# Cross-attention with a routed feed-forward on one core: the feed-forward two token tiles behind the attention, a third x2 buffer, row maxima and one product of k's rotation kept in PSUM

## What is computed

```python
x = x + xattn(layernorm(x), ctx, ctx, pos, Wq, Wk, Wv, Wo)
x = x + ffn(layernorm(x), A, B, Wq_w, keys)

# xattn: 32 query heads of 16, 8 key/value heads (each used by 4 query heads), 16 batches of 64 x 64 scores
q = rope(query @ Wq);  k = rope(key @ Wk);  v = value @ Wv        # rope(a) = a*cos + rotate_half(a)*sin
out = softmax(q k^T / sqrt(16)) v @ Wo

# ffn: a low-rank feed-forward with a router over 64 experts of rank 8, 16 of them taken
scores = (x @ Wq_w.T) @ keys.T
gate   = softmax over the 16 largest scores, zero elsewhere       # (token, 64)
out    = ((x @ A.T) * gate, each gate value for 8 columns) @ B.T * 2
```

## Time and profile before

| | before |
|---|---|
| median of 3 runs | 194.94 us (194.22 to 195.06) |
| the profiled execution's own time | 194.51 us |
| its span, first to last instruction | 192.8 us |
| TensorE (PE) busy | 173.4 us, 90% |
| VectorE (DVE) busy | 151.0 us, 78% |
| ScalarE (ACT) busy | 89.9 us, 47% |
| GpSimd (POOL) busy | 86.8 us, 45% |
| moved by DMA | 11.3 MB, most of it in the first 25 us |
| chain that ended last, by engine | TensorE 51%, VectorE 29%, waiting for nothing visible 12%, ScalarE 5% |

### The profile page before, as it was taken

How to read it: one execution, slowest core, us unless ns; L and a number is a source line. 1 busy time by engine, 2 the same in 40 slices (tenths; PEclk the granted TensorE clock), 3 DMA queues, 4 the chain that set the end, 5 groups by cost and what they waited for, 6 DMA issues and landing times.

```text
span 192.8 us, 4096 instructions
## 1 busy us (share of the span) xinstructions
PE 173.4 (90%) x1446; PEld 130.6 (68%) x1446; DVE 151.0 (78%) x391; ACT 89.9 (47%) x206; POOL 86.8 (45%) x109
## 2 busy tenths in 40 slices
PE   7998899968997999989997999989999896788884
PEld 2656474745984878667975878667866784567764
DVE  2588959997899887988799597986798497645671
ACT  3767789537252741546352732456233614412310
POOL 5698888699489105740267104810363020220300
PEclk9999999999999999999999999999999999999999
DMA  5999501020010302001010100010000100000102
GB/s 187 327 389 401 231 2 56 2 51 7 3 54 0 109 3 56 0 3 54 3 56 0 58 0 0 2 53 5 3 0 0 58 0 0 5 2 0 54 37 75
DMA packets 5332, 11.32 MB, mean 59 GB/s; under 512 B 688, under 2 KB 944, under 8 KB 5056
## 3 DMA queue, kind: packets, MB, share of 16 engines
q1 hardware_dynamic: 5024, 10.79, 16.0%
q10 hardware_dynamic: 288, 0.27, 0.4%
HBM read 8.95 MB, written 2.10 MB: 57 GB/s over the span
## 4 chain that ended last, share of the span: by engine, by line
PE 51%; DVE 29%; issue 12%; ACT 5%; DVEq 0%; ACTq 0%
PE ps_w L1013 8%; DVE neg_top L734 8%; PE ps_w L1008 6%; PE ps_t L1021 6%; PE ps_w L1009 5%; PE ps_s L1104 4%; DVE m_split L744 3%; PE ps_s L1087 3%; PE ps_t L1026 3%; PE ps_w L1163 3%; DVE o_s L752 3%; DVE q_a L717 2%; DVE o_t L761 2%; DVE q_b L719 2%; PE ps_w L1155 2%
## 5 line engine op out<-in xcount | busy, mean ns | idle before, releaser
L313 POOL TENSOR_TENSOR late<-late,gate 128x512 f32<-128x512 f32 x7 | 8.0, 1145 | 48.8 <-issue 32.1
L734 DVE TENSOR_REDUCE neg_top<-ps_s 128x8 f32<-128x512 f32 x32 | 19.8, 676 | 0.7 <-PE ps_s L1068 0.7
L298 POOL TENSOR_TENSOR oT_lo<-o_n,oT_hi 128x512 fp32r<-128x512 f32 x8 | 10.3, 1285 | 21.0 <-ACT oT_hi L491 21.0
L483 ACT ACTIVATE eT<-ps_s 128x512 f32<-128x512 f32 x32 | 17.0, 600 | 4.2 <-PE ps_s L1093 4.2
L1008 PE MATMUL ps_w<-am_hi,x2T_hi 128*128 128x288 f32 x52 | 15.4, 319 | 1.6 <-ACT x2T_hi L504 1.6
L1008 PE MATMUL ps_w<-b_hi,zT_hi 128*128 128x512 f32 (+1 forms) x32 | 12.8, 405 | 3.9 <-DVE q_b L719 2.0
L1009 PE MATMUL ps_w<-am_lo,x2T_hi 128*128 128x288 f32 x52 | 14.2, 296 | 0.0
L1008 PE MATMUL ps_w<-wo_hi,oT_hi 128*128 128x512 f32 x32 | 13.3, 414 | 0.9 <-ACT oT_hi L491 0.8
L476 ACT ACTIVATE mT<-ps_t 128x256 fp32r<-128x256 f32 x8 | 3.1, 384 | 23.2 <-PE ps_t L1077 23.2
L1009 PE MATMUL ps_w<-wo_lo,oT_hi 128*128 128x512 f32 x32 | 12.6, 395 | 0.0
L1009 PE MATMUL ps_w<-b_lo,zT_hi 128*128 128x512 f32 (+1 forms) x32 | 12.1, 381 | 0.0
(11 more groups left out here) (187 smaller groups left out, 528.2 us busy)
## 6 DMA issues: line engine op xcount, KB each, us to landing
x_sb<-x SPq DMA_DIRECT2D x8, 256.0 KB, 6.6
cT_in<-cT SPq DMA_DIRECT2D x7, 256.0 KB, 2.9
out<-res SPq DMA_DIRECT2D x7, 256.0 KB, 2.0
wq_sb<-wq SPq DMA_DIRECT2D x4, 256.0 KB, 6.2
late<-wo SPq DMA_DIRECT2D x1, 1024.0 KB, 8.4
am_sb<-aT SPq DMA_DIRECT2D x1, 1024.0 KB, 7.7
b_sb<-bT SPq DMA_DIRECT2D x1, 1024.0 KB, 6.3
wkv_sb<-wkv SPq DMA_DIRECT2D x1, 512.0 KB, 4.5
```

What stands on the lines that cost most here:

```text
L298: pool.tensor_tensor(oT_lo[:], o_n[:].rearrange("p (b r q) -> p r b q", b=2, r=REP), oT_hi[:].bitcast(F32), ALU.subtract).then_inc(oT_lo_o ...
L483: act.activation(eT[:, c].rearrange("p b n -> p (b n)"), ps_s[:, c, :], ACT.Exp)\
L734: dve.tensor_reduce(neg_top[:, :, b, HALF_H * half:HALF_H * (half + 1)], ps_s[:, 2 * (1 - b) + half, :].rearrange("p (r h k) -> p r h k", ...
```

## The change

The computation stays the same. `step(i)` on all engines now runs the feed-forward of token f = i - 2 (none in step 1); g = i - 1 is the token whose x2 is turned and split in that step. `last()` therefore has four feed-forwards (z = 4, a = 5, m = 6, l = 7) instead of three, in a new order on each engine. x2 gets a third buffer in the part of `wq_sb` that raw q no longer needs. x2 is turned into bank `ps_t1` (before: `ps_t0`); some banks of the last tokens differ. `neg_top` becomes 32 columns of the scores' own third bank, with the order of the two inner indices swapped, and the second maximum waits for the first; `k_a` becomes 128 free columns of `ps_w1`. In `first()` on ScalarE `x_raw(0)` comes earlier. Two splits of B move on GpSimd. The stores of tokens 0 and 1 move behind later loads. 12 warming multiplications instead of 18. On GpSimd `last()` only gains `gated(z)` in front; `gated(a)` and `deviation2(m)` stand before `o_low(l)` as they did. On ScalarE, in `last()` not shown below, `q_high(l)` comes behind `z_first(z)`, `o_high(m)` behind the exponentials of l and `expert_exps(a)`, then `o_high(l)`, `x2_centre(m)`, `z_second(a)`, `x2_high(m)`, `z_high(a)`.

```diff
-WARM = 18
+WARM = 12
...
-        k_a, k_b, k_r = sb("k_a", [P, KV]), sb("k_b", [P, KV]), sb("k_r", [P, KV])
+        k_b, k_r = sb("k_b", [P, KV]), sb("k_r", [P, KV])
...
-        neg_top = sb("neg_top", [P, 2, 2, KVH])
...
+        neg_top = ps_s[:, 2, 0:4 * KVH].rearrange("p (b h r) -> p b h r", b=2, r=2)
+        k_a = ps_w1[:, 2 * KV:3 * KV]
...
         def x2_of(t):
-            return x2[:, t % 2, :] if t < T - 1 else xh[:]
+            return (x2[:, 0, :], x2[:, 1, :], wq_sb[:, 0, :])[t % 3]
+
+        def x2T_of(t):
+            return (x2T_hi, x2T_lo) if t < T - 1 else (xT_hi, xT_lo)
+
+        def x2T_bank(t):
+            return ps_t0 if t == T - 1 else ps_t1
+
+        def y_bank(t):
+            return ps_w1[:] if t < T - 1 else ps_s[:, 2, :]
 
...
             load_c(4)
             load_x(6)
             load_c(5)
-            store(0)
             load_x(7)
             load_c(6)
-            store(1)
+            store(0)
             load_c(7)
-            for t in range(2, T - 1):
+            for t in range(1, T - 1):
...
-                split_lo(b_lo, b_sb, b_hi, b_h, b_l, 0)
                 rotated_q(2)
                 c_low(3)
-                split_lo(b_lo, b_sb, b_hi, b_h, b_l, 1)
+                k_blocks(2, 0)
+                k_blocks(2, 1)
 
             def step(i):
-                f, n, p = i - 1, i + 1, i + 2
+                f, n, p = i - 2, i + 1, i + 2
                 if p + 1 < T:
                     deviation1(p + 1)
-                deviation2(f)
-                if i == 1:
-                    k_blocks(n, 0)
-                    k_blocks(n, 1)
-                gated(f)
-                if i == 1:
-                    split_lo(b_lo, b_sb, b_hi, b_h, b_l, 2)
-                    split_lo(b_lo, b_sb, b_hi, b_h, b_l, 3)
+                if f >= 0:
+                    gated(f)
+                else:
+                    for k in range(2):
+                        split_lo(b_lo, b_sb, b_hi, b_h, b_l, k)
+                deviation2(i - 1)
                 o_low(i)
                 k_blocks(p, 0)
                 k_blocks(p, 1)
+                rotated_q(p)
                 if p + 1 < T:
                     c_low(p + 1)
-                rotated_q(p)
+                if f < 0:
+                    for k in range(2, DK):
+                        split_lo(b_lo, b_sb, b_hi, b_h, b_l, k)
 
             def last():
-                l, m, a = T - 1, T - 2, T - 3
+                l, m, a, z = T - 1, T - 2, T - 3, T - 4
+                gated(z)
                 deviation2(a)
...
+                split_hi(wkv_hi, wkv_sb, wkv_h, 0)
+                split_hi(wkv_hi, wkv_sb, wkv_h, 1)
+                x_raw(0)
+                split_hi(wkv_hi, wkv_sb, wkv_h, 2)
+                split_hi(wkv_hi, wkv_sb, wkv_h, 3)
...
             def step(i):
-                f, n, p = i - 1, i + 1, i + 2
-                x2_high(f)
+                f, g, n, p = i - 2, i - 1, i + 1, i + 2
                 for c in range(PAIRS - 1):
                     exps(i, c)
-                expert_scores(f)
+                if f >= 0:
+                    expert_scores(f)
                 exps(i, PAIRS - 1)
-                z_first(f)
-                expert_exps(f)
+                if f >= 0:
+                    z_first(f)
+                    expert_exps(f)
+                    z_second(f)
+                x2_high(g)
                 q_high(n)
-                z_second(f)
                 values_out(p)
                 o_high(i)
                 k_high(p)
-                z_high(f)
+                if f >= 0:
+                    z_high(f)
                 if p + 1 < T:
...
-                    dve.tensor_reduce(neg_top[:, :, b, HALF_H * half:HALF_H * (half + 1)],
-                                      ps_s[:, 2 * (1 - b) + half, :].rearrange("p (r h k) -> p r h k", r=2, h=HALF_H),
+                    if b == 0 and half == 1:
+                        dve.wait_ge(max_ok, 4 * t + 1)
+                    dve.tensor_reduce(neg_top[:, b, HALF_H * half:HALF_H * (half + 1), :],
+                                      ps_s[:, 2 * (1 - b) + half, :].rearrange("p (r h k) -> p h r k", r=2, h=HALF_H),
                                       AX.X, ALU.max, negate=True).then_inc(max_ok, 1)
...
             def step(i):
-                f, n, p = i - 1, i + 1, i + 2
-                x2_low(f)
+                f, g, n, p = i - 2, i - 1, i + 1, i + 2
                 if p > RAW:
                     x_low(p)
                 if p + 2 < T:
                     statistics1(p + 2)
-                route(f)
-                if i == 1:
-                    q_low(n)
-                    attend(i)
-                else:
-                    attend(i, lambda: q_low(n))
+                if f >= 0:
+                    route(f)
+                x2_low(g)
+                attend(i, lambda: q_low(n))
                 rotate_k(p)
                 top(n, 0)
                 top(n, 1)
                 k_low(p)
                 rotate_q(p)
                 m_parts(n)
-                z_low(f)
+                if f >= 0:
+                    z_low(f)
                 residual(i)
                 statistics2(i)
-                result(f)
+                if f >= 0:
+                    result(f)
 
             def last():
-                l, m, a = T - 1, T - 2, T - 3
+                l, m, a, z = T - 1, T - 2, T - 3, T - 4
+
+                def maxima():
+                    top(l, 0)
+                    top(l, 1)
+                    m_parts(l)
+                    z_low(z)
+
+                route(z)
                 x2_low(a)
                 q_low(l)
-                attend(m)
-                top(l, 0)
-                top(l, 1)
-                m_parts(l)
-                route(a, lambda: residual(m))
+                attend(m, maxima)
+                route(a)
+                result(z)
+                attend(l)
+                residual(m)
                 statistics2(m)
-                attend(l)
-                z_low(a)
                 x2_low(m)
                 residual(l)
                 x2_centre_last()
                 statistics2(l)
+                z_low(a)
                 route(m, lambda: x2_low(l))
                 result(a)
...
             def step(i):
-                f, n, p = i - 1, i + 1, i + 2
-                if i == 1:
-                    turned_scores(i)
-                    pe.wait_ge(q_rot, 6)
-                    project_q(p, [0])
-                    pe.wait_ge(x_lo_ok, 1)
-                    turn_x2(f)
+                f, g, n, p = i - 2, i - 1, i + 1, i + 2
+                turned_scores(i)
+                if f >= 0:
+                    pe.wait_ge(x2_ok, i)
+                    project_down(f, 0)
+                    if f >= 1:
+                        pe.wait_ge(res_ok, f)
+                    else:
+                        pe.wait_ge(q_rot, 2 * p)
+                    project_q(p, [0, 1])
+                    pe.wait_ge(z_ok, 2 * f + 1)
+                    project_down(f, 1)
+                    turn_x2(g)
                 else:
-                    pe.wait_ge(mT_ok, i + 1)
-                    turn_x2(f)
-                    turned_scores(i)
-                pe.wait_ge(x2_ok, i)
-                project_down(f, 0)
-                if i >= 2:
-                    pe.wait_ge(res_ok, f)
-                    project_q(p, [0])
-                project_q(p, [1])
+                    pe.wait_ge(q_rot, 2 * p)
+                    project_q(p, [0, 1, 2])
+                    turn_x2(g)
                 values(i)
-                pe.wait_ge(x2T_lo_ok, i)
                 turn_q(n)
-                pe.wait_ge(z_ok, 2 * f + 1)
-                project_down(f, 1)
-                project_q(p, [2])
-                pe.wait_ge(z_ok, 2 * i)
+                if f >= 0:
+                    pe.wait_ge(z_ok, 2 * f + 2)
+                else:
+                    pe.wait_ge(x2_ok, i)
                 project_kv(p)
+                if f >= 0:
+                    project_q(p, [2])
                 scores(n, 0)
                 scores(n, 1)
-                pe.wait_ge(kT_lo_ok, n + 1)
-                turn_zg(f)
+                pe.wait_ge(x2T_lo_ok, i)
+                if f >= 0:
+                    turn_zg(f)
                 project_q(p, [3]).then_inc(q_ps, 1)
-                pe.wait_ge(qT_lo_ok, n + 1)
                 turn_k(p)
                 pe.wait_ge(v_st_ok, p + 1)
                 project_out(i)
-                pe.wait_ge(q_rot, 2 * p + 2)
-                up_high(f)
+                if f >= 0:
+                    pe.wait_ge(q_rot, 2 * p + 2)
+                    up_high(f)
                 pe.wait_ge(kT_lo_ok, p + 1)
                 turn_m(n)
-                up_low(f)
+                if f >= 0:
+                    up_low(f)
                 if p + 1 < T:
                     turn_xh(p + 1)
...
```

(58 more changed lines are left out.)

113 lines of the change are left out of this document (48 added, 65 removed).

## The result

The kernel after takes **184.56 us** (median of 4 runs, 184.47 to 184.78) against 194.78 us for the kernel before, timed beside it (4 runs, 194.22 to 195.06): ratio **0.948**, 95% interval 0.9456 to 0.9505.

What follows compares the result with a forecast made beforehand. TensorE was taken as the fullest engine, its waits caused by late VectorE operations. The span 192.8 - 3.1 (start) - 6.8 (step 1) - 3.4 (steady steps) + 4.9 (end) = 184.4 us gave 186.5 us, range 181.0 to 191.0.

Steps and rivals of the forecast that it cites:

- The stall of SBUF inputs: VectorE operations with SBUF inputs wait out GpSimd's instruction; PSUM inputs save 1.07 us in `k_r`, 2.0 in `m_parts`.
- The rival in which VectorE waits whatever it reads: VectorE waits for GpSimd's instruction even with PSUM inputs; 21.9 us a step, 198.1 us in all; chance 0.05.
- Writing into PSUM: VectorE's five writes of maxima and `k_a`: 0 to 0.1 us each, taken at 0; chance of dearer 0.06.
- The new wait: On VectorE, the second maximum waiting for the first costs 0.1 us a step.
- The cast: On VectorE, reading PSUM costs the cast 0.07 us more than its best in SBUF, 0.5 over eight tokens.
- Steady step: Steps 2 to 5: the loop through VectorE and TensorE sets 20.4 us a step, -3.4 us in all.
- TensorE is all that is left: Rival: TensorE's own work sets steps at 19.9 us, step 1 takes 15.5, total 181 us; chance 0.15.
- Step 1: Without feed-forward, step 1 goes from 23.82 to 17.0 us (13.1 work, 3.9 stalls): -6.8 us.
- The start: Up to token 1's turned scores: fewer warming multiplications, earlier `x_raw(0)` and shorter `m_parts` give -3.1 us.
- the warming: At the start, 12 warming multiplications instead of 18 bring `turn_xh` 1.1 us earlier at most.
- The end: `last` with a fourth feed-forward: +6.8 us of TensorE work, about 1.9 filled into idle time, net +4.9 us.
- The splits of b: GpSimd's four moved splits are hidden, as b is first needed in step 2, or cost one split of 1.3 us.

Runs made afterwards that it cites:

- psum_only: Kernel before, in its own order, with `k_a` and the maxima in PSUM and the second maximum waiting for the first: 187.33 us, ratio 0.9624 to before.
- order_only: Kernel after with `k_a` and the maxima (`neg_top`) back in SBUF, all orders as changed: 188.02 us, ratio 0.967 to before.
- pe_minus: Kernel after with three of the twelve multiplications of `project_out` left out in tokens 2 to 5: 184.23 us, ratio 0.9479.
- dve_plus2: Kernel after with three extra waiting additions of 128 elements in `attend` on VectorE, tokens 2 to 5: 187.85 us, ratio 0.9653.
- loop_c: `end_b` with `rotate_q` on VectorE between the two pairs of maxima in steps 2 to 5, and behind `m_parts` in step 1: 180.98 us, ratio 0.9316.
- psum_only_2: The same kernel as `psum_only`, looked at once more in a single run: 186.05 us.
- end_b: Kernel after with `project_out(7)` begun ahead of `turn_x2(6)`, `o_low(7)` ahead of `gated(5)` and `deviation2(6)`, `q_low(7)` inside `route(4)`: 182.08 us, ratio 0.9358.
- loop_d: `loop_c` with the last two splits of b on GpSimd moved behind `deviation1` of step 2: 180.33 us, ratio 0.9247.

## Why the prediction was right, and where it was not

The total and every sign held; the sum was too small by 1.9 of 10.3. Part of that nearness is luck: the gains of step 1 and of the steady steps were 3.8 too small, those of the start and the end 1.9 too good, and the two cancel by half.

*The stall of SBUF inputs*: right. Each of the three operations falls to 0.28 to 0.29 in all eight instances, and `psum_only` shows it with the neighbour unchanged. The rival in which VectorE waits whatever it reads is out. Writing into PSUM, bounded at 0 to 0.1 and taken at 0, has a small price where only the place differs: from `order_only` to after the median of `k_a` goes from 0.252 to 0.270 and that of a maximum from 0.682 to 0.690, 0.05 a token in all. The new wait was put at 0.1: four maxima take 2.47 in before, 2.61 with the wait alone (`order_only`) and 2.62 with both. The cast takes 0.28 from PSUM and 0.21 at its best in SBUF (`order_only`), the 0.07 of the forecast. The Trainium skill (VectorE: DVE Perf Modes, Why PSUM operands drop a tier) says that a PSUM operand takes the faster mode away, and the trace agrees.

*Steady step*: right in kind, mis-sized. The loop sets it, as `pe_minus` and `dve_plus2` show, and the chain on VectorE was forecast at 8.7 and is 8.56 (81.17 to 89.73). TensorE's part of the loop was forecast at 11.5 and is 19.65 - 8.56 = 11.1, semaphores included, where I added 0.2 for those and for rounding: from `up_high` to the turned scores it takes 3.64 (3.86 forecast), from there to the end of the values 7.39 (7.61). The whole step is 0.73 shorter than forecast, 2.8 over four. The other floor was off too: I took TensorE alone at 19.9, adding up 1.5 of waits and drains; `loop_c` shows 19.40. So the rival "TensorE is all that is left", worked out at 19.9 a step, was nearer in its number than in its reason: 19.67 is the loop, 0.27 above TensorE. The forecast also gave the PSUM tiles and the order a share each of the step. That was wrong: `k_r`'s 1.07 was counted for PSUM, but the order alone takes `k_r` out of GpSimd's way, and either part alone brings the step to about 0.3 or less above TensorE's 19.40, below which neither could go.

*Step 1*: forecast 13.1 of work and 3.9 of stalls, measured 13.55 busy and 2.4 idle. The waits are 0.64 for the exponentials (1.2 forecast), 1.38 for `m_split` (1.6) and 0.26 before the scores; before `turn_k`, put at 1.0, there is none.

*The start*: -3.1 forecast, -2.4 measured. The stalls of `m_parts` and `k_r` were its larger part, as forecast (1.8 by `order_only`). The mis-sized term is the warming, 1.1: it was read from one execution and followed to `turn_xh(0)`, not on to the load that holds token 1, and behind that load it earns nothing. `psum_only_2`, with 18 warming multiplications and `x_raw(0)` still behind the sines, starts token 1 at 38.03, also 26.79 behind the statistics that wait for the load: against that execution neither part of the change at the start gains. They can gain only against one like the earlier trace rows, in which TensorE comes to token 1 late.

*The end*: +4.9 forecast, +6.1 measured. The +6.8 of work, the filled 2.17 and the wait for `oT_lo` (1.1 forecast, 0.65) were there. The missing 1.2 is the wait for `x_c(6)`, 1.60, that I hadn't in the list; what I didn't do is follow VectorE's order behind `attend(7)`. `end_b` shows that most of these waits come from the hand-written order and not from the dependences: other orders alone shorten `last` by 2.4.

*The splits of b*: called hidden. In after they are so by slack: VectorE waits 2.02 in step 2 for the operations behind them, and that doesn't reach TensorE. `loop_c` used the slack up, and there their place costs 0.8 (`loop_d`).

## What to carry to other kernels

Two remedies for one stall don't add up: when either brings the step down near the bound behind it, the second earns only where that bound isn't near (here the start and the first step), so work out the next bound before crediting both. A small wait for another engine on an engine that looks 100% busy can still be the bound; to decide, take work off the full engine and see whether the step moves. And where an order is written by hand, list for each engine what stands behind each moved block: `x_c(6)` at the end and the splits of b in `loop_c` were both the same thing, an instruction whose inputs were ready but which stood behind another in its engine's order.
